# Cross attention: a step's second rounding of queries and keys ahead of the second exponentials, and both remainders in a row

## The chip, the cores and the metric

The kernel runs on one core of one Trainium2 chip. The metric is the time of one execution on the device, in microseconds (us).

## The reference

One transformer block on x (32 batches of 256 tokens, width 256) with a context of 32 x 256 tokens of width 192, all in float32:

```python
h = _layernorm(x, ln1_g, ln1_b)
x = _attention(h, h, sa_wq, sa_wk, sa_wv, sa_wo, sa_bo) + x
h = _layernorm(x, ln2_g, ln2_b)
x = _attention(h, cond_emb, ca_wq, ca_wk, ca_wv, ca_wo, ca_bo) + x
h = _layernorm(x, ln3_g, ln3_b)
p = h @ ff_w1 + ff_b1
a, gate = (p[..., :D_FF], p[..., D_FF:])
h = a * jax.nn.gelu(gate, approximate=False) @ ff_w2 + ff_b2
return h + x
```

`_attention` has 16 heads of 64: q, k and v are projections, the softmax of q k / 8 over the 256 keys weighs v, and the result goes through wo.

## The kernel before

**Rounds and steps.** Each engine has its program written out by hand, and semaphores tie them together. The kernel runs 32 rounds of self attention (`sa`), one for each batch, then 32 of cross attention (`ca`), then the feed-forward part. A round t has four steps, n = 0 to 3, and a step attends to two pairs of heads, pairs 2n and 2n+1. Rounds overlap: while round t ("cur") computes its scores, the output projection of batch t-1 ("prv") and the first projections of batch t+1 ("nxt") are done too. `STEP_UNITS` says which projections (units) stand in which step:

```python
    ((("v", 0, 0), "cur"), (("qk", 2), "cur"), (("qk", 3), "cur"), (("v", 0, 1), "cur")),
    ((("qk", 4), "cur"), (("qk", 5), "cur"), (("wo", 0), "prv")),
    ((("v", 1, 0), "cur"), (("x",), "nxt"), (("qk", 6), "cur"), (("qk", 7), "cur"), (("v", 1, 1), "cur")),
    ((("qk", 0), "nxt"), (("qk", 1), "nxt"), (("wo", 1), "prv")),
```

So every step projects two pairs of queries and keys, and the scores of the next step need both.

**Precision.** A float32 product is made of three products of rounded parts. Each operand is split into its rounding (`_hi`, taken by ScalarE's copy into fp32r) and the remainder (`_lo`, a subtraction on VectorE or GpSimd). For queries and keys: TensorE leaves them in a PSUM bank of `unit_ps`, ScalarE writes `qk_hi` (L887), VectorE `qk_lo` (L1054).

**A step, engine by engine.**

- TensorE: scores of both pairs (`scores`, L605; it waits for the remainders of both pairs), the step's units (`run_unit`, L592), then the weighted sum of an earlier step's values (`attend`, L617).
- VectorE (`attention_iteration` from L1130 on): maximum of the first pair (L1029), transpose of the previous step's second pair (L1043), maximum of the second pair, inverse of the first pair's sums (L1034), remainder of an earlier attended result (L1049), remainder of the first projected pair (L1054), in some steps norm statistics or the transpose of rows (L1020), inverse of the second pair's sums, remainder of the second projected pair (L1054), transpose of this step's first pair. At the end of step 2 come the remainders of the next batch's normed input hT (`x_remainder`, L1067) and of the context's first half (`context_remainder`, L1071, cross attention only). Both subtract one SBUF tensor from another.
- ScalarE: rounding of an earlier attended result (L858), exponentials of the first pair (L849, four rows each with its sum), the units "evacuated early" (`evacuated_early`: the first two of the qk and v units in an even step, the first in an odd one), exponentials of the second pair, the other units. Step 1 ends with the scaling of rows_in to hT (L840) and the norm (L827), step 2 with the copies of context and hT (L874, L876). In each step it issues four of the 16 moves of blocks (L865).
- GpSimd: normalises each pair's probabilities when its sums are inverted (L1259), once in a round the second half of the context's remainder (L1268), behind the normalisation of pair 5, and small work.
- SyncE issues the DMAs: for each step 12 moves of `blocks` to `pT` (L522), behind both transposes of that step (its wait is at L519; the second pair's transpose stands in the next step of VectorE), and once in a round the loads of ctx_in, rows_in and x_res and the stores of x_out and of the rows. rows_in (L507) is the normed input of the next batch, transposed through DRAM. In cross attention's rounds 34 to 36 four loads of feed-forward weights are added.

Of the kernel before, what the change touches and what calls it, by code (L numbers as in the profile page):

```python
# [46 lines left out]
STEP_UNITS = (  # L47
# [5 lines that stand above are left out]
# [44 lines left out]
def attended_before(t, n, parts):  # L97

    if n:
        return attended(t, n - 1, parts)  # L100
    return (t - 1, 1) if "prv" in parts else None
# [58 lines left out]
def block_kernel(nc, x, ctx, ln1_g, ln1_b, ln2_g, ln2_b, ln3_g, ln3_b, sa_wq, sa_wk, sa_wv, sa_wo, sa_bo,  # L160
# [4 lines left out]
    with stack:  # L165
# [170 lines left out]
        ca = Pass("ca", 1, x_sa, x_ca, True, (ca_wq, ca_wk, ca_wv, ca_wo), B, 4)  # L336
# [4 lines left out]
        def pass_of(b, home):  # L341

            return home if not isinstance(b, int) else sa if b < B else ca
# [62 lines left out]
        def norms(t, parts, home):  # L406

            if parts == FILL:
                return [(at, sa, 0, 0)]
            if parts == START:  # L410
                return [(at, sa, 1, 0), (at, sa, 2, 2)]
            if parts == LAST:
                return [(ff, ff, 0, 0)]
            return [] if isinstance(t, int) and t + 2 >= TOTAL else [(at, pass_of(t + 2, home), t + 2, 0)]
# [368 lines left out]
        def _(act):  # L783
# [70 lines left out]
            def attended_hi(b, n):  # L854
                act.wait_ge(at.o_full, b * STEPS + n + 1)
                if n % 2 == 0:
                    at_least(act, at.wo_full, 2 * b - 2 + n // 2 + 1)
                nc.scalar.copy(a_hi[:, 2 * n:2 * n + 2, :], o_ps[:]).then_inc(at.a_hi_done, 1)  # L858
# [16 lines left out]
                act.wait_ge(at.h_done, b + 1)  # L875
                nc.scalar.copy(hT_hi[:, 0, :, :], hT[:]).then_inc(at.x_hi, 1)  # L876

            def evacuated_early(n):

                return [unit for unit in STEP_UNITS[n] if unit[0][0] in ("qk", "v")][:2 if n % 2 == 0 else 1]  # L880

            def split_unit(t, unit, part):
                b = batch_of(t, part)
# [27 lines left out]
            def end_attention():  # L911
                last = TOTAL - 1
                attended_hi(last, 1)
                act.wait_ge(at.qk_full, TOTAL * PAIRS)
                split_ff_weight(0)
                move_blocks(last, 3, ca)
                split_ff_weight(1)
                act.wait_ge(at.v_full, 4 * TOTAL)
                rows_hi(0, 0)
                split_ff_weight(2)  # L920
                attended_hi(last, 2)
                act.wait_ge(param_ld, PARAMS)
                gelu(0, 0)
                gelu(0, 1)
                hidden_hi(0, 0)
                attended_hi(last, 3)

            def attention_iteration(t, parts, home):
                if parts == DRAIN:
                    end_attention()  # L930
                    return
                for sems, ph, b, s in norms(t, parts, home):
                    if s == 0 and parts != FILL:
                        load_rows(sems, ph, b)
                for n in range(STEPS):
                    units = [unit for unit in STEP_UNITS[n] if unit[1] in parts]
                    if behind := attended_before(t, n, parts):
                        attended_hi(*behind)
                    if n == 3 and parts == FILL:
                        split_inputs(t + 1, home)  # L940
                    for p in hi_first(t, n):
                        split_piece(p)
                    if "cur" in parts:
                        exponentials(t, 2 * n)
                    for unit in units:
                        if unit in evacuated_early(n):
                            split_unit(t, *unit)
                    if "cur" in parts:
                        exponentials(t, 2 * n + 1)
                    for unit in units:  # L950
                        if unit not in evacuated_early(n):
                            split_unit(t, *unit)
                    if n == 1 and blocks_next(t, parts):
                        scale_rows(t + 1, home)
                    for sems, ph, b, s in norms(t, parts, home):
                        if n == (2 if isinstance(t, int) and t == 1 else s + 1):
                            if sems is ff:

                                act.wait_ge(at.row_blocks, TOTAL - WHOLE)
                            normalise(sems, b)  # L960
                        if n == 1 and s == 2:
                            load_rows(sems, ph, b)
                    if n == 2 and "nxt" in parts and parts != FILL:
                        split_inputs(t + 1, home)
                    if ready := moved(t, n, parts):
                        move_blocks(*ready, home)
                    for p in hi_last(t, n):
                        split_piece(p)
# [17 lines left out]
        def _(dve):  # L986
# [145 lines left out]
            def attention_iteration(t, parts, home):  # L1132
                if parts == DRAIN:
                    end_attention()
                    return
                if isinstance(t, int) and t == 1:
                    dve.wait_ge(param_ld, PARAMS)

                    for a in (ln_gain, ln_bias):
                        nc.vector.tensor_scalar(a[:, ca.norm, :], a[:, ca.norm, :], SCALE, None, ALU.mult).then_inc(rows_scaled, 1)  # L1140
                for n in range(STEPS):
                    pairs = [(batch_of(t, part), unit[1]) for unit, part in STEP_UNITS[n] if unit[0] == "qk" and part in parts]
                    for sems, ph, b, s in norms(t, parts, home):
                        if n == s + 1:
                            dve.wait_ge(sems.bn_done, b + 1)
                    if "cur" in parts:
                        maxima(t, 2 * n)
                    if behind := moved(t, n, parts):
                        transpose_blocks(behind[0], 2 * behind[1] + 1, home)
                    if "cur" in parts:  # L1150
                        maxima(t, 2 * n + 1)
                    for sems, ph, b, s in norms(t, parts, home):
                        if n == s + 1:
                            norm_moments(sems)
                    if n == 3 and parts == FILL:
                        x_remainder(t + 1)
                    if parts != FILL:
                        for p in lo_vector(t, n):
                            split_queries(p)
                    if "cur" in parts:  # L1160
                        invert_sums(t, 2 * n)
                    if n == 2 and "nxt" in parts and by_tensor(t + 1):
                        if parts == FILL:
                            dve.wait_ge(norm_ld, 16 * 2)
                        scale_inputs(t + 1, home)
                    if behind := attended_before(t, n, parts):
                        attended_lo(*behind)
                    for pair in pairs[:1]:
                        qk_remainders(*pair)
                    for sems, ph, b, s in norms(t, parts, home):  # L1170
                        if n == s:
                            norm_statistics(sems, b)
                    if n == 3 and blocks_ahead(t, parts):
                        transpose_rows(at, t + 2)
                    if "cur" in parts:
                        invert_sums(t, 2 * n + 1)
                    for pair in pairs[1:]:
                        qk_remainders(*pair)
                    if "cur" in parts:
                        transpose_blocks(t, 2 * n, home)  # L1180
                    if n == 2 and "nxt" in parts and parts != FILL:
                        x_remainder(t + 1)
                        if pass_of(t + 1, home).has_ctx:
                            context_remainder(t + 1)
                    if n % 2 and "prv" in parts:
                        project_out(t - 1, n // 2)
                    if parts == FILL:
                        for p in lo_vector(t, n):
                            split_queries(p)
# [160 lines left out]
```

## Time and profile before

| | |
|---|---|
| median of 3 runs | 2939.59 us (2935.07 to 2942.47) |
| profiled execution, own time | 2934.73 us |
| its span | 2932.9 us |
| TensorE busy | 2880.7 us, 98% |
| VectorE busy | 2278.4 us, 78% |
| ScalarE busy | 1911.4 us, 65% |
| GpSimd busy | 1472.5 us, 50% |
| mean granted TensorE clock | 0.996 |

The profile is one execution. Its page gives each engine's busy share, the queues, the chain of work that ended last and the costliest groups of instructions. The views of the trace used below are the timeline (each row: start and duration in us, engine, line, operation, output<-inputs, how many; in brackets the idle time ahead of it and what ended it), and the waits (who waited for whom, us in total, how often, the longest). "PE" is TensorE, "DVE" VectorE, "ACT" ScalarE, "POOL" GpSimd; "SPq" and "ACTq" are DMA issues of SyncE and ScalarE. The duration of an issue is the time in which it holds its sequencer, not that of the transfer. Ends of matmuls are modelled, so TensorE is read by starts.

### The profile page before, as it was taken

To read this page: it belongs to the slowest core of one execution; us is meant where nothing else is said; L and a number is where in the kernel's file an instruction comes from. 1 tells how busy PE (TensorE), PEld (TensorE's weight loads), DVE (VectorE), ACT (ScalarE), POOL (GpSimd) and SP (SyncE) were. 2 spreads that over 40 slices of the span, in tenths; PEclk is the share of its full clock that TensorE was granted. 3 is DMA by queue.
4 is the path that set the end of the run, shared out by engine and by line. 5 is a ranking of instruction groups with operands and counts; after the bars stand their busy time and mean duration, and the time that the engine had idled before them with its cause. 6 is when DMAs were issued, how large, how long until landed. Compare 5 with 4: busy or idle time off the path is not lost.

```text
span 2932.9 us, 76346 instructions
## 1 busy us (share of the span) xinstructions
PE 2880.7 (98%) x25278; PEld 2510.3 (86%) x25278; DVE 2278.4 (78%) x3495; ACT 1911.4 (65%) x6041; POOL 1472.5 (50%) x1310
## 2 busy tenths in 40 slices
PE   8999999999999999999999999999999999999999
PEld 7878888888888888887888888888888889999999
DVE  6878888888888888887888888888888865555554
ACT  6667766666666677876777777777777754444443
POOL 5444444444444444754555555555555545455454
PEclk9999999999999999999999999999999999999999
DMA  5665555555555555566656656666665532222222
GB/s 145 168 170 155 149 149 149 149 149 150 147 147 149 149 149 149 152 164 175 166 159 159 161 159 161 161 161 162 161 162 160 152 109 72 86 75 73 88 72 62
DMA packets 535575, 413.37 MB, mean 141 GB/s; under 512 B 171201, under 2 KB 520769, under 8 KB 535489
## 3 DMA queue, kind: packets, MB, share of 16 engines
q1 hardware_dynamic: 443424, 328.31, 41.1%
q10 hardware_dynamic: 92064, 83.96, 11.2%
q8 instruction: 48, 0.79, 0.1%
q14 instruction: 39, 0.31, 0.0%
HBM read 94.52 MB, written 49.02 MB: 49 GB/s over the span
## 4 chain that ended last, share of the span: by engine, by line
PE 58%; SPq 14%; ACT 12%; DVE 8%; issue 5%; ACTq 3%; DMA 1%; DVEq 0%; POOL 0%; POOLq 0%
PE unit_ps L592 31%; SPq L522 12%; PE s_ps L592 12%; PE o_ps L617 8%; ACT probs L849 8%; PE s_ps L605 7%; ACTq L865 3%; DVE blocks L1043 3%; DVE neg_max L1029 3%; ACT qk_hi L887 3%; DVE hT_lo L1071 1%; DVE hT_lo L1067 1%; DVE qk_lo L1054 1%; ACT x_n L827 1%; DMA rows_in<-rows_t_dram 1%
## 5 line engine op out<-in xcount | busy, mean ns | idle before, releaser
L1259 POOL TENSOR_TENSOR probs<-probs,row_inv 128x1024 f32<-128x1024 f32 x512 | 967.7, 1895 | 956.8 <-DVE row_inv L1034 956.7
L849 ACT ACTIVATE probs<-s_ps,neg_max 128x256 f32<-128x256 f32 x2048 | 952.8, 491 | 266.2 <-DVE neg_max L1029 265.9
L1029 DVE TENSOR_REDUCE neg_max<-s_ps 128x4 f32<-128x1024 f32 x512 | 615.7, 1203 | 72.0 <-PE s_ps L605 71.4
L1043 DVE STREAM_TRANSPOSE blocks<-probs 128x1024 f32<-128x1024 f32 x512 | 632.4, 1235 | 21.3 <-POOL probs L1259 20.9
L592 PE MATMUL unit_ps<-hT_hi,w_hi 128*128 128x256 f32 x2048 | 572.6, 283 | 2.1 <-DVE hT L1024 1.6
L592 PE MATMUL unit_ps<-hT_hi,w_lo 128*128 128x256 f32 x2048 | 555.4, 277 | 0.0
L617 PE MATMUL o_ps<-pT,v_f 128*64 128x256 f32 x4096 | 501.8, 387 | 5.8 <-DMA pT<-blocks 4.6
L592 PE MATMUL unit_ps<-hT_lo,w_hi 128*128 128x256 f32 x1792 | 497.0, 277 | 0.0
L849 ACT ACTIVATION_READ_ACCUMULATOR probs<-s_ps,neg_max 128x1 f32 x2048 | 450.9, 220 | 0.0
L592 PE MATMUL unit_ps<-w_hi,a_hi 128*128 128x256 f32 x1536 | 438.3, 285 | 1.4 <-POOL a_lo L1274 1.0
L592 PE MATMUL unit_ps<-w_hi,a_lo 128*128 128x256 f32 x1536 | 435.0, 283 | 0.0
L592 PE MATMUL unit_ps<-w_lo,a_hi 128*128 128x256 f32 x1536 | 429.9, 280 | 0.0
L1054 DVE TENSOR_TENSOR qk_lo<-unit_ps,qk_hi 128x512 fp32r<-128x512 f32 x512 | 352.6, 689 | 99.4 <-ACT qk_hi L887 95.3
L617 PEld LDWEIGHTS o_ps<-pT,v_f 128*64 128x64 f32 x4096 | 272.8, 137 | 182.2 <-issue 49.4
L592 PEld LDWEIGHTS unit_ps<-hT_hi,w_hi 128*128 128x128 f32 x2048 | 385.1, 188 | 20.7 <-DVE hT L1024 2.0
L592 PEld LDWEIGHTS unit_ps<-hT_hi,w_lo 128*128 128x128 f32 x2048 | 385.0, 188 | 0.0
L858 ACT CAST a_hi<-o_ps 128x512 fp32r<-128x512 f32 x256 | 150.4, 588 | 339.9 <-issue 138.7
L592 PEld LDWEIGHTS unit_ps<-hT_lo,w_hi 128*128 128x128 f32 x1792 | 336.9, 188 | 5.7
L605 PE MATMUL s_ps<-qk_hi 64*128 64x256 f32 x2048 | 316.7, 305 | 20.7 <-DVE qk_lo L1054 18.2
L1274 POOL TENSOR_TENSOR a_lo<-probs,a_hi 128x256 fp32r<-128x256 f32 x256 | 190.0, 747 | 266.7 <-ACT a_hi L905 265.0
L900 ACT ACTIVATE probs<-s_ps,b_col 128x256 f32<-128x256 f32 x256 | 121.8, 476 | 303.4 <-PE s_ps L592 303.4
L887 ACT CAST qk_hi<-unit_ps 128x512 fp32r<-128x512 f32 x512 | 315.0, 615 | 3.7 <-PE unit_ps L592 3.6
(73 smaller groups left out, 6009.7 us busy)
## 6 DMA issues: line engine op xcount, KB each, us to landing
pT<-blocks SPq DMA_DIRECT2D x3072, 64.0 KB, 2.0
pT<-blocks ACTq DMA_DIRECT2D x1024, 64.0 KB, 2.1
rows_t_dram<-row_blocks SPq DMA_DIRECT2D x91, 256.0 KB, 2.4
rows_in<-rows_t_dram SPq DMA_DIRECT2D x91, 256.0 KB, 2.9
x_res<-in_x_dram SPq DMA_DIRECT2D x32, 256.0 KB, 2.7
x_sa_dram<-x_out SPq DMA_DIRECT2D x32, 256.0 KB, 2.2
x_ln<-x_sa_dram ACTq DMA_DIRECT2D x32, 256.0 KB, 3.2
ctx_in<-in_ctx_dram SPq DMA_DIRECT2D x32, 256.0 KB, 2.8
```

The source lines that it names most:

```text
L522: sp.dma_start(pT[j * BLK:(j + 1) * BLK, n % 2, :, i, :], blocks[i * BLK:(i + 1) * BLK, n % 2, :, j, :]).then_inc(landed(b, n, home)[0], 16)
L592: last = nc.tensor.matmul(dst, a, b, start=start and n == 0, stop=stop and n == len(terms) - 1)
L605: last = nc.tensor.matmul(s_ps[:, m % 2, hd, it * S:(it + 1) * S], q[part, r, 0, rows], k[part, r, 1, :], start=n == 0, stop=n == 2)
L617: last = nc.tensor.matmul(o_ps[part, i, :], v_f[:, jt, 2 * (2 * n + i) + hd, :], p[:, jt, hd], start=jt == 0, stop=jt == IT - 1)
L849: op = nc.scalar.activation(probs[:, m % 2, r, :], s_ps[:, m % 2, r // IT, r % IT * S:(r % IT + 1) * S], ACT.Exp, bias=neg_max[:, m % RING ...
L858: nc.scalar.copy(a_hi[:, 2 * n:2 * n + 2, :], o_ps[:]).then_inc(at.a_hi_done, 1)
L887: nc.scalar.copy(qk_hi[:, unit[1] % RING, :, :], bank.rearrange("p (a s) -> p a s", a=2)).then_inc(at.qk_hi, 1)
L1029: nc.vector.tensor_reduce(neg_max[:, m % RING, :], s_ps[:, m % 2, :, :].rearrange("p h (i j) -> p (h i) j", j=S), AX_X, ALU.max, negate=Tr ...
L1043: nc.vector.transpose(blocks[:, n % 2, m % 2, :, :].rearrange("p b (j r c) -> p r j b c", j=IT, c=BLK), probs[:, m % 2, :, :].rearrange("p ...
L1054: nc.vector.tensor_tensor(qk_lo[:, m % RING, :, :], unit_ps[:, bank_of(("qk", m)), :].rearrange("p (a s) -> p a s", a=2), f32(qk_hi[:, m % ...
L1259: nc.gpsimd.tensor_tensor(probs[:, m % 2, :, :], probs[:, m % 2, :, :], row_inv[:, m % RING, :].unsqueeze(2).broadcast_to([P, ROWS, S]), A ...
L1274: nc.gpsimd.tensor_tensor(a_lo[:, m, :], hid[:, m % 2, :], f32(a_hi[:, m, :]), ALU.subtract).then_inc(ff.u_lo, 1)
```

## The change

In rounds of cross attention, one more qk unit counts as early. ScalarE rounds the second projected pair of a step behind the first and ahead of the second exponentials; VectorE takes the remainder of the second pair right behind that of the first, ahead of norm statistics, the transpose of rows and the inverse of the second pair's sums. Self attention is left as it is, and so are TensorE, GpSimd and SyncE. Behind L878 line numbers grow by two, and by three in what follows the second edit.

```diff
@@ -875,9 +875,11 @@
-            def evacuated_early(n):
-
-                return [unit for unit in STEP_UNITS[n] if unit[0][0] in ("qk", "v")][:2 if n % 2 == 0 else 1]
+            def evacuated_early(t, n, home):
+
+
+                units = [unit for unit in STEP_UNITS[n] if unit[0][0] in ("qk", "v")]
+                return units[:(2 if n % 2 == 0 else 1) + (1 if pass_of(t, home) is ca else 0)]
@@ -1165,7 +1167,8 @@
-                    for pair in pairs[:1]:
+                    early = 2 if "cur" in parts and pass_of(t, home) is ca else 1
+                    for pair in pairs[:early]:
                         qk_remainders(*pair)
@@ -1174,7 +1177,7 @@
-                    for pair in pairs[1:]:
+                    for pair in pairs[early:]:
                         qk_remainders(*pair)
```

ScalarE in step 2 of a cross attention round, behind the exponentials of pair 4, before (the register instructions hold a value to wait for):

```order
L893 COPY v_f<-unit_ps 128x512
L886 REGISTER_ALU
L887 CAST qk_hi<-unit_ps 128x512
L849 ACTIVATE probs,row_sum<-s_ps,neg_max 128x256 x4
L886 REGISTER_ALU
L887 CAST qk_hi<-unit_ps 128x512
L891 REGISTER_ALU
L893 COPY v_f<-unit_ps 128x512
```

and now:

```order
L895 COPY v_f<-unit_ps 128x512
L888 REGISTER_ALU
L889 CAST qk_hi<-unit_ps 128x512
L888 REGISTER_ALU
L889 CAST qk_hi<-unit_ps 128x512
L849 ACTIVATE probs,row_sum<-s_ps,neg_max 128x256 x4
L893 REGISTER_ALU
L895 COPY v_f<-unit_ps 128x512
```

The second rounding (pair 7) has moved ahead of the four exponentials of pair 5; v stays behind them.

VectorE in the same step, from the remainder of an attended result (`a_lo`) to the remainder of the next input (`hT_lo`), before:

```order
L1049 TENSOR_TENSOR a_lo<-o_ps,a_hi 128x512
L1053 REGISTER_ALU
L1054 TENSOR_TENSOR qk_lo<-unit_ps,qk_hi 128x512
L1034 RECIPROCAL row_inv<-row_sum 128x4
L1053 REGISTER_ALU
L1054 TENSOR_TENSOR qk_lo<-unit_ps,qk_hi 128x512
L1042 ISA
L1043 STREAM_TRANSPOSE blocks<-probs 128x4x2x4x32
L1066 REGISTER_ALU
L1067 TENSOR_TENSOR hT_lo<-hT,hT_hi 128x512
```

and now:

```order
L1051 TENSOR_TENSOR a_lo<-o_ps,a_hi 128x512
L1055 REGISTER_ALU
L1056 TENSOR_TENSOR qk_lo<-unit_ps,qk_hi 128x512
L1055 REGISTER_ALU
L1056 TENSOR_TENSOR qk_lo<-unit_ps,qk_hi 128x512
L1036 RECIPROCAL row_inv<-row_sum 128x4
L1044 ISA
L1045 STREAM_TRANSPOSE blocks<-probs 128x4x2x4x32
L1068 REGISTER_ALU
L1069 TENSOR_TENSOR hT_lo<-hT,hT_hi 128x512
```

The remainder of the second pair has moved ahead of the inverse of the second sums, which now stands right in front of the transpose of the first pair (`blocks`).

## Rows read from the trace of the kernel before

**Rows 1.** TensorE timeline, cross attention, step ends: start us, us, engine, line, op.
```profile
1705.56 1.95 PE L617 MATMUL o_ps<-pT,v_f 128*64 128x256 f32 x16
1707.44 0.39 PE L605 MATMUL s_ps<-qk_hi 64*128 64x256 f32 x2
...
1714.10 1.95 PE L617 MATMUL o_ps<-pT,v_f 128*64 128x256 f32 x16
1716.27 0.39 PE L605 MATMUL s_ps<-qk_hi 64*128 64x256 f32 x2 [0.23 <-DVE qk_lo L1054]
...
1732.24 1.95 PE L617 MATMUL o_ps<-pT,v_f 128*64 128x256 f32 x16
1734.41 0.38 PE L605 MATMUL s_ps<-qk_hi 64*128 64x256 f32 x2 [0.22 <-DVE qk_lo L1054]
```

**Rows 2.** SyncE's queue, one round of cross attention, timeline.
```profile
1702.87 0.39 SPq L512 DMA_DIRECT2D ctx_in<-in_ctx_dram  x1
1703.46 0.37 SPq L507 DMA_DIRECT2D rows_in<-rows_t_dram  x1
1704.03 15.94 SPq L522 DMA_DIRECT2D pT<-blocks  x24
1720.18 0.42 SPq L543 DMA_DIRECT2D x_res<-x_sa_dram  x1
1721.17 7.97 SPq L522 DMA_DIRECT2D pT<-blocks  x12
...
1738.91 0.39 SPq L512 DMA_DIRECT2D ctx_in<-in_ctx_dram  x1
```

**Rows 3.** Waits of SyncE, 1200 to 2365 us: total, times, longest us.
```profile
SPq L519 <- DVE blocks L1043: 13.9, 28, 1.7
```

**Rows 4.** SyncE's queue, timeline of a round that also loads feed-forward weights.
```profile
1334.81 0.46 SPq L512 DMA_DIRECT2D ctx_in<-in_ctx_dram  x1
...
1373.86 0.46 SPq L512 DMA_DIRECT2D ctx_in<-in_ctx_dram  x1
```

**Rows 5.** ScalarE timeline, step 1's end and step 2 of cross attention.
```profile
1706.75 0.64 ACT L840 ACTIVATE hT<-rows_in,ln_bias,ln_gain 128x256 f32<-128x256 f32 x1 [1.27 <-DMA rows_in<-rows_t_dram]
...
1710.27 0.48 ACT L849 ACTIVATE probs<-s_ps,neg_max 128x256 f32<-128x256 f32 x1
...
1713.02 0.53 ACT L849 ACTIVATE probs<-s_ps,neg_max 128x256 f32<-128x256 f32 x1
...
1714.84 0.65 ACT L887 CAST qk_hi<-unit_ps 128x512 fp32r<-128x512 f32 x1
...
1715.30 0.67 ACT L893 COPY v_f<-unit_ps 128x512 f32<-128x512 f32 x1
...
1716.30 0.71 ACT L876 CAST hT_hi<-hT 128x512 fp32r<-128x512 f32 x1
```

**Rows 6.** VectorE timeline, end of step 2 and start of step 3.
```profile
1716.13 1.24 DVE L1043 STREAM_TRANSPOSE blocks<-probs 128x1024 f32<-128x1024 f32 x1
1717.29 0.65 DVE L1067 TENSOR_TENSOR hT_lo<-hT,hT_hi 128x512 fp32r<-128x512 f32 x1
1717.86 0.96 DVE L1071 TENSOR_TENSOR hT_lo<-ctx_in,hT_hi 128x256 fp32r<-128x256 f32 x1
1718.73 1.21 DVE L1029 TENSOR_REDUCE neg_max<-s_ps 128x4 f32<-128x1024 f32 x1
1719.87 1.23 DVE L1043 STREAM_TRANSPOSE blocks<-probs 128x1024 f32<-128x1024 f32 x1
```

**Rows 7.** GpSimd timeline, same stretch.
```profile
1715.30 1.90 POOL L1259 TENSOR_TENSOR probs<-probs,row_inv 128x1024 f32<-128x1024 f32 x1 [0.91 <-DVE row_inv L1034]
1717.36 1.18 POOL L1268 TENSOR_TENSOR hT_hi<-ctx_in,hT_hi 64x256 fp32r<-64x256 f32 x1 [0.16 <-POOL probs L1259]
```

**Rows 8.** Timeline of VectorE and GpSimd near the start of self attention.
```profile
45.47 2.37 POOL L1254 TENSOR_TENSOR w_lo<-w_stage,w_hi 128x1024 fp32r<-128x1024 f32 x1
...
45.89 2.50 DVE L1067 TENSOR_TENSOR hT_lo<-hT,hT_hi 128x512 fp32r<-128x512 f32 x1
```

More of the change, by code:

```diff
@@ L945, in attention_iteration @@
                     for unit in units:
-                        if unit in evacuated_early(n):
+                        if unit in evacuated_early(t, n, home):
                             split_unit(t, *unit)
@@ L950, in attention_iteration @@
                     for unit in units:
-                        if unit not in evacuated_early(n):
+                        if unit not in evacuated_early(t, n, home):
                             split_unit(t, *unit)
```

## The prediction

> **What bounds the kernel now.** The change touches only the 32 rounds of cross attention (one per batch, some 36 us each, four steps a round, n = 0 to 3), so I read that stretch engine by engine and asked which engine is never idle there.
>
> First TensorE, because the page shows it as the busiest. A step ends with the attend product (L617) and the next begins with the scores (L605). Where nothing is waited for, the scores start 1.88 us behind the attend (1707.44 less 1705.56). At two other step ends they start 2.17 us behind it, and the wait printed there is for qk_lo, the remainder that VectorE takes last in a step [rows 1]. That is 0.29 us twice a round. The fourth step end shows no wait as long as these, so I count it between 0 and 0.29 and take the middle. TensorE loses some 0.58 + 0.15 = 0.73 us a round for remainders that come late. This is what the change goes after, and 32 x 0.73 = 23.4 us is what it could give if TensorE set the pace.
>
> Second SyncE's queue, because each step moves its transposed blocks by 12 DMAs from there. One round lies between two ctx_in loads: 1738.91 - 1702.87 = 36.04 us. In it the issues stand one behind the other, with gaps of 0.20 us (1703.83 to 1704.03), except one: from the end of the x_res issue, 1720.60, to 1721.17 there are 0.57 us, so SyncE waits 0.37 [rows 2]. The wait view names what for: VectorE's blocks (L1043), 28 times in cross attention, 13.9 us in all, and nothing else [rows 3]. SyncE thus has 36.04 - 0.37 = 35.67 us of its own work a round, and TensorE without its waits would need 36.04 - 0.73 = 35.31. **SyncE, not TensorE, is the longer.** A second sign: a round that has four more loads on SyncE lasts 1373.86 - 1334.81 = 39.05 us [rows 4], though no engine computes anything more in it.
>
> Third, what the one wait of SyncE hangs on. It is a ring. SyncE issues rows_in at 1703.46 [rows 2]; ScalarE has been idle for it and scales it at 1706.75, issues its own four moves and starts the exponentials of pair 4 at 1710.27 [rows 5]. Then follow, without idle time, two roundings, the exponentials of pair 5 (1713.02), the rounding of pair 7 (1714.84), v (1715.30), and the copies of context and hT (the last from 1716.30) [rows 5]. VectorE subtracts hT's rounding at 1717.29, then the context's, takes the maximum of pair 6 at 1718.73 and transposes pair 5 at 1719.87, to 1721.10 [rows 6]. SyncE goes on at 1721.17 [rows 2], and after fixed work comes to the next rows_in. Nothing of TensorE's sets a time in this ring. So a round is SyncE's work plus how late that transpose of pair 5 comes, counted from rows_in.
>
> **The change, part by part.**
>
> (1) ScalarE in step 2: the rounding of pair 7 goes ahead of the exponentials of pair 5. It occupied the slot 1714.84 to 1715.30, 0.46 us [rows 5]. The exponentials start 0.46 later, and v and everything behind it stay where they are, since the same work stands ahead of them. Steps 3, 0 and 1 get the same swap, but it only moves work inside stretches where ScalarE waits for VectorE or rows_in at the next step's start; I cost it at nothing, the cover being ScalarE's idle time (1.27 us ahead of rows_in) [rows 5]. If the cover goes, each step costs up to 0.46.
>
> (2) VectorE takes both remainders in a row, in time in which it waited for the exponentials. In step 2 the transpose of pair 4 then no longer stands behind the remainder of pair 7. It starts as soon as the later sums are inverted, some 0.5 us sooner than at 1716.13. TensorE's waits of [rows 1] go.
>
> (3) What this does for the ring. hT's remainder was held by that transpose, not by its input: ScalarE's copy ended at 1716.30 + 0.71 = 1717.01 [rows 5], VectorE began at 1717.29 [rows 6]. Read this far, the remainder could start at about 1717.06, 0.23 sooner, and every round would be 0.23 shorter.
>
> (4) What stands against it. GpSimd normalises pair 5 when its sums are inverted, from 1715.30 to 1717.20, and the remainder began 0.09 us behind its end [rows 6, 7]. With the exponentials 0.46 later, GpSimd works from 1715.76 to 1717.66, across 1717.06. Do the two work at the same time? The trace has such a case: at 45.89 the same instruction at L1067 meets a GpSimd subtraction that runs from 45.47 to 47.84. It lasts 2.50 us in place of 0.65, and ends at 48.39, 0.55 behind GpSimd [rows 6, 8]. The context's remainder shows the same in every round: 256 columns take 0.96 us where 512 take 0.65, and they end at 1718.82, 0.28 behind GpSimd's own context instruction (1717.36 + 1.18 = 1718.54) [rows 6, 7]. So the two take turns. The Trainium skill, "SBUF — State Buffer", section "Who interferes with whom", says that a VectorE instruction with two SBUF inputs contends with a GpSimd instruction that reads SBUF, and that the one that comes second blocks for the whole instruction. The trace agrees with it (2.50 us in place of 0.65). By that rule the ring gets longer; without it, it would get 0.23 us shorter.
>
> The sum for a round: hT's remainder is held to 1717.66, ends at 1717.66 + 0.55 = 1718.21 instead of 1717.94, which is **0.27 us later**. GpSimd's context instruction waits for it, VectorE's context remainder waits for that, as now, so the maximum of pair 6, the transpose of pair 5 and SyncE's next move are all 0.27 later. SyncE's wait grows from 0.37 to 0.64.
>
> For the kernel: the 28 rounds with a wait of SyncE for that transpose [rows 3] give 28 x 0.27 = 7.6 us. In the others SyncE is late anyway and covers it. TensorE's 23.4 us are not paid out: it comes to its next product earlier and waits there, since SyncE's pace holds rows_in and with it v. Only behind the last round can it keep a little of its lead, about one step end's wait or two; I take 0.6. Sum: +7.0 us on the profiled execution's own 2934.73, so 2941.7, a quarter of a per cent. The median of the runs shown, 2939.59, lies 4.9 us above that execution; the same +7.0 there gives **2946.6 us**. What a measurement of this kernel can tell from no change is about 0.3%, 8.8 us: my forecast is no change that can be told, on the slow side.
>
> Bounds of the unknown. The price of the turn-taking lies between -0.23 (none) and +0.43 a round (below), the nearest row being the 2.50 us of [rows 8], which is the same instruction, so I take its 0.55.
>
> **Rivals.**
>
> *The remainder runs beside the normalisation.* Then part (3) holds: 28 x 0.23 = 6.4 us less, 2933.2. It can't give more than SyncE's whole wait, 13.9 us [rows 3]. For it: the GpSimd instruction of [rows 8] is another than the normalisation. Against it: both read two tensors. Chance 0.15.
>
> *TensorE sets the pace after all.* Then all waits of [rows 1] are gained: 2939.6 - 23.4 = 2916.2. For it: 98% busy on the page, the waits are real, and SyncE's issues could shrink. Against it: [rows 2 to 4]. Chance 0.06.
>
> *Slower beyond doubt.* GpSimd's context instruction follows its normalisation by 0.16 us [rows 7]. If it gets its turn ahead of the waiting remainder, it runs from 1717.82 for the 0.60 that it takes alone (1718.54 less 1717.94), to 1718.42; then hT's remainder to 1718.97, the context's to 1719.25 instead of 1718.82, 0.43 later. 28 x 0.43 = 12.0 us: 2951.6. What decides is who gets in within those 0.16 us; the waiting one should. Chance 0.12.
>
> *The halves cancel and nothing moves*: 2939.6, chance 0.07. The diff moves exactly what it names, so I give nothing to its not doing so.
>
> **How the numbers follow.** The forecast has 0.60. The range takes in the first rival, the forecast and the third with the spread of the runs shown (some 3.7 us to either side): 2929 to 2955; the TensorE case stays outside. Faster by over 0.3%: 0.06, and a third of the first rival, together 0.11. Slower by over 0.3%: nearly all of the third rival and a fifth of the forecast, 0.24. The rest, 0.65, is within.
>
> **What would show it.** In the profile after: no wait of the scores for qk_lo in cross attention; TensorE idle instead ahead of the v product, for ScalarE's v_f. The remainder of hT recorded at some 1.2 us instead of 0.65, ending 0.55 behind GpSimd's normalisation. Rounds of 36.3 us. SyncE's waits for blocks some 0.64 each. If hT's remainder stays at 0.65 and rounds are 35.8, step (4) is wrong; if rounds are 35.3, the reading of SyncE is wrong; if SyncE has no wait and rounds are longer, its issues got slower, which I did not foresee.

## The result and the profile after

| | before | after |
|---|---|---|
| median of 17 runs each | 2939.55 us (2935.07 to 2945.67) | 2947.96 us (2942.78 to 2951.2) |
| ratio after/before, 95% interval | | 1.0027 (1.002 to 1.0033) |
| span of the profiled execution | 2932.9 us | 2943.5 us |
| granted TensorE clock | 0.996 | 0.997 |
| mean round, rows_in to rows_in, 1450 to 2250 us (22 rounds before, 21 after) | 36.01 us | 36.29 us |

The kernel got slower, by a little less than the 0.3% that I took as what can be told; with 17 runs on each side the interval excludes 1. The forecast was 2946.6.

SyncE's queue in one round after, the answer to [rows 2] (columns: start, duration, engine and line, operation, number of issues):

```profile
1709.63 0.39 SPq L512 DMA_DIRECT2D ctx_in<-in_ctx_dram  x1
1710.22 0.37 SPq L507 DMA_DIRECT2D rows_in<-rows_t_dram  x1
1710.79 15.90 SPq L522 DMA_DIRECT2D pT<-blocks  x24
1726.90 0.42 SPq L543 DMA_DIRECT2D x_res<-x_sa_dram  x1
1728.18 7.88 SPq L522 DMA_DIRECT2D pT<-blocks  x12
...
1745.84 0.39 SPq L512 DMA_DIRECT2D ctx_in<-in_ctx_dram  x1
```

The only hole is again behind x_res: 1728.18 - (1726.90 + 0.42) = 0.86 us, of which 0.20 is the usual gap. SyncE waits 0.66 us where it waited 0.37. The round is 1745.84 - 1709.63 = 36.21 us.

VectorE in that step, the answer to [rows 6] (in brackets the idle time ahead and what ended it):

```profile
1722.23 0.18 DVE L1036 RECIPROCAL row_inv<-row_sum 128x4 f32<-128x4 f32 x1 [1.04 <-ACT probs L849]
1722.38 1.25 DVE L1045 STREAM_TRANSPOSE blocks<-probs 128x1024 f32<-128x1024 f32 x1
1723.75 1.18 DVE L1069 TENSOR_TENSOR hT_lo<-hT,hT_hi 128x512 fp32r<-128x512 f32 x1
1724.86 0.96 DVE L1073 TENSOR_TENSOR hT_lo<-ctx_in,hT_hi 128x256 fp32r<-128x256 f32 x1
1725.74 1.21 DVE L1031 TENSOR_REDUCE neg_max<-s_ps 128x4 f32<-128x1024 f32 x1
1726.87 1.23 DVE L1045 STREAM_TRANSPOSE blocks<-probs 128x1024 f32<-128x1024 f32 x1
```

and GpSimd, the answer to [rows 7]:

```profile
1722.49 1.89 POOL L1262 TENSOR_TENSOR probs<-probs,row_inv 128x1024 f32<-128x1024 f32 x1 [1.39 <-DVE row_inv L1036]
1724.54 0.99 POOL L1271 TENSOR_TENSOR hT_hi<-ctx_in,hT_hi 64x256 fp32r<-64x256 f32 x1 [0.16 <-POOL probs L1262]
```

hT's remainder now begins at 1723.75, inside the normalisation (1722.49 to 1724.38). It lasts 1.18 us instead of 0.65 and ends at 1724.93, 0.55 us behind the normalisation's end, as the case in [rows 8] did. GpSimd's context instruction, VectorE's context remainder, the maximum and the transpose of pair 5 follow. Counted from the start of the exponentials of pair 4, the steady rounds show GpSimd's normalisation of pair 5 starting 0.48 us later (5.52 instead of 5.04), hT's remainder starting 0.24 sooner (6.78 instead of 7.02) and the maximum of pair 6 starting 0.29 later (8.76 instead of 8.47). The end of the remainder goes with the end of the normalisation: it lies 0.55 us behind it now and lay 0.74 behind it before, so of the 0.48 us there remain 0.29.

TensorE at a step's end and ahead of v, the answer to [rows 1]:

```profile
1711.57 1.95 PE L617 MATMUL o_ps<-pT,v_f 128*64 128x256 f32 x16
1713.45 0.38 PE L605 MATMUL s_ps<-qk_hi 64*128 64x256 f32 x2
...
1719.44 0.50 PE L592 MATMUL unit_ps<-w_hi,hT_hi 128*128 128x512 f32 x1 [0.43 <-ACT v_f L895]
```

The scores now start 1.88 us behind the attend product, the undisturbed distance of [rows 1], at every step end of cross attention but two. Summed over all step ends, what the distance exceeds its least fell from some 21 us to under 0.1. That leaves out one step end before (0.93 us) and two after (1.18 us each), all in rounds that also load feed-forward weights: there the attend product itself takes 2.88 and 3.13 us instead of 1.95. None of this reached the time: TensorE waits ahead of v instead. The waits of TensorE and of SyncE's queue from 1450 to 2250 us, 22 rounds (columns: total, times, longest), after:

```profile
PE unit_ps L592 <- ACT v_f L895: 11.8, 22, 0.9
...
SPq L519 <- DVE blocks L1045: 16.1, 22, 1.3
```

and the same rows before:

```profile
PE s_ps L605 <- DVE qk_lo L1054: 8.9, 42, 0.2
...
PE unit_ps L592 <- ACT v_f L893: 0.2, 1, 0.2
...
SPq L519 <- DVE blocks L1043: 9.7, 22, 1.0
```

SyncE's total wait grew by 6.4 us in 22 rounds, 0.29 a round.

Where the 10.6 us between the two profiled spans lie follows from SyncE's ctx_in loads (starts of the first round's, the seventh's and a late one's; before, then after):

```profile
1184.85 0.59 SPq L512 DMA_DIRECT2D ctx_in<-in_ctx_dram  x1
...
1412.76 0.39 SPq L512 DMA_DIRECT2D ctx_in<-in_ctx_dram  x1
...
2278.68 0.39 SPq L512 DMA_DIRECT2D ctx_in<-in_ctx_dram  x1
```

```profile
1186.35 0.59 SPq L512 DMA_DIRECT2D ctx_in<-in_ctx_dram  x1
...
1418.00 0.39 SPq L512 DMA_DIRECT2D ctx_in<-in_ctx_dram  x1
...
2290.09 0.39 SPq L512 DMA_DIRECT2D ctx_in<-in_ctx_dram  x1
```

Ahead of cross attention +1.5 us (nothing is changed there; in the seven other profiled kernels that leave ctx_in's load on SyncE this stretch ends between 1182.4 and 1186.8 us, so I take it for the spread between executions); six early rounds 231.65 instead of 227.91, +3.7; 24 steady rounds 872.09 instead of 865.92, +6.2, or 0.26 each; behind them -0.8.

### The profile page after: what moved, and what is told of

The parts are those of the page before. It is cut to its first block, busy times and chain, and to the rows that moved or that the text cites. A ratio compares the mean times of both kernels' runs of the same rounds, so it can differ in the third digit from the quotient of the medians.

```text
span 2943.5 us, 76346 instructions
## 1 busy us (share of the span) xinstructions
PE 2884.1 (98%) x25278; PEld 2510.7 (85%) x25278; DVE 2290.2 (78%) x3495; ACT 1909.9 (65%) x6041; POOL 1465.2 (50%) x1310
## 4 chain that ended last, share of the span: by engine, by line
PE 50%; SPq 23%; ACT 8%; issue 7%; DVE 4%; DMA 3%; ACTq 3%; POOL 2%; POOLq 0%; DVEq 0%
PE unit_ps L592 26%; SPq L522 20%; PE s_ps L592 12%; PE o_ps L617 7%; PE s_ps L605 6%; ACT probs L849 4%; DMA rows_in<-rows_t_dram 2%; ACTq L865 2%; DVE blocks L1045 2%; DVE neg_max L1031 1%; ACT qk_hi L889 1%; POOL probs L1262 1%; DVE hT_lo L1073 1%; ACT x_n L827 1%; ACT v_f L895 1%
## 5 line engine op out<-in xcount | busy, mean ns | idle before, releaser
L1056 DVE TENSOR_TENSOR qk_lo<-unit_ps,qk_hi 128x512 fp32r<-128x512 f32 x512 | 341.0, 685 | 62.8 <-ACT qk_hi L889 58.8
L1090 DVE SCALAR_TENSOR_TENSOR probs<-s_ps,b_col,probs 128x256 f32<-128x256 f32 x256 | 123.3, 482 | 244.7 <-ACT probs L902 242.5
```

Source lines behind the costliest of these rows:

```text
L1056: nc.vector.tensor_tensor(qk_lo[:, m % RING, :, :], unit_ps[:, bank_of(("qk", m)), :].rearrange("p (a s) -> p a s", a=2), f32(qk_hi[:, m % ...
L1090: nc.vector.scalar_tensor_tensor(hid[:, m % 2, :], s_ps[:, m % 4 // 2, m % 2, 0:S], b1_col[:, m:m + 1], gate[:, m % 2, :], ALU.add, ALU.mu ...
```

## The experiments

The theory was the ring of the prediction, lengthened by the turn-taking of hT's remainder with GpSimd's normalisation. The rivals: the longer rounds come from another of the four steps, or SyncE is not what sets the pace. The times of before in the four groups of runs were 2936.98 (first three kernels), 2939.33 (next four), 2940.17 (next four) and 2940.76 us (last). All ratios are to before.

**Is step 2 the place? The change in steps 3, 0 and 1 alone, and in step 2 alone.** In the functions of the edit, for the first (`n == 2` for the second):

```diff
-                return units[:(2 if n % 2 == 0 else 1) + (1 if pass_of(t, home) is ca else 0)]
+                return units[:(2 if n % 2 == 0 else 1) + (1 if pass_of(t, home) is ca and n != 2 else 0)]
...
-                    early = 2 if "cur" in parts and pass_of(t, home) is ca else 1
+                    early = 2 if "cur" in parts and pass_of(t, home) is ca and n != 2 else 1
```

> The change in steps 0, 1 and 3 of cross attention alone; step 2 as before. Theory (the price comes from step 2, where GpSimd's normalisation of pair 5 slides across VectorE's remainder of hT): nothing in the ring moves, rounds of 36.0 us, SyncE's wait 0.37, hT's remainder 0.65 long; time as the kernel before, ratio 0.999 to 1.001. Rival (each step that swaps its second rounding pays for the later exponentials): three quarters of the loss of 8 us, ratio about 1.002.

Measured: 2929.6 us, ratio 0.9975 (0.9964 to 0.9986), mean round 35.74 us. No lengthening, as expected, but a gain of 7.4 us where I expected none.

> The change in step 2 alone. Theory: the whole loss, rounds of 36.3 us, hT's remainder recorded at some 1.2 us, ratio 1.002 to 1.004. Rival (every step pays its part): a quarter of the loss, ratio about 1.0007.

Measured: 2945.98 us, ratio 1.0032 (1.002 to 1.0043), mean round 36.37, SyncE's wait 16.7 us in 22 rounds. The whole loss is in step 2. The two halves don't add up: -7.4 + 9.0 = +1.6 us, and the full change costs 8.4. The mean rounds say the same: -0.27 and +0.36 us alone, +0.28 together.

**Is it the turn-taking?** In cross attention the remainder of hT reads, in place of the SBUF tensor hT, the PSUM bank of pair 7. In this kernel hT_lo is therefore not hT's remainder; engine, shape, place in the order and the waits of the other engines are the same.

```diff
+                if home is not None and pass_of(b, home).has_ctx:
+                    nc.vector.tensor_tensor(hT_lo[:, 0, :, :],
+                                            unit_ps[:, bank_of(("qk", 7)), :].rearrange("p (a s) -> p a s", a=2),
+                                            f32(hT_hi[:, 0, :, :]), ALU.subtract).then_inc(at.x_lo, 1)
+                    return
                 nc.vector.tensor_tensor(hT_lo[:, 0, :, :], hT[:], f32(hT_hi[:, 0, :, :]), ALU.subtract).then_inc(at.x_lo, 1)
```

> The change whole, but in cross attention VectorE's remainder of hT takes its first input from a PSUM bank (what the projection of pair 7 left there) instead of from hT, so that it has one SBUF input; its size is the same. The remainder it writes is therefore not that of hT. Theory (two SBUF inputs and GpSimd take turns): it starts at 6.78 us behind the exponentials of pair 4 as in the changed kernel and now lasts 0.65 us beside the normalisation; the context's remainder gets in right behind the normalisation; the maximum of pair 6 comes some 0.8 us sooner than in the kernel before (7.6 to 7.7 instead of 8.47), SyncE's wait goes, rounds fall to SyncE's own 35.7 us: ratio 0.996 to 0.998. Rival (the later normalisation or the later exponentials delay the ring in another way): it stays at 1.002 to 1.003.

Measured: 2920.79 us, ratio 0.9946 (0.9932 to 0.9959), mean round 35.38: a larger gain than expected. VectorE:

```profile
1712.93 1.25 DVE L1045 STREAM_TRANSPOSE blocks<-probs 128x1024 f32<-128x1024 f32 x1
1714.30 0.69 DVE L1070 TENSOR_TENSOR hT_lo<-unit_ps,hT_hi 128x512 fp32r<-128x512 f32 x1
1714.91 0.42 DVE L1078 TENSOR_TENSOR hT_lo<-ctx_in,hT_hi 128x256 fp32r<-128x256 f32 x1
1715.24 1.22 DVE L1031 TENSOR_REDUCE neg_max<-s_ps 128x4 f32<-128x1024 f32 x1
```

and GpSimd:

```profile
1713.05 1.90 POOL L1267 TENSOR_TENSOR probs<-probs,row_inv 128x1024 f32<-128x1024 f32 x1 [1.39 <-DVE row_inv L1036]
1715.10 0.82 POOL L1276 TENSOR_TENSOR hT_hi<-ctx_in,hT_hi 64x256 fp32r<-64x256 f32 x1 [0.16 <-POOL probs L1267]
```

The same subtraction over the same normalisation (1713.05 to 1714.95) lasts 0.69 us and ends at 1714.99, when only one of its inputs is in SBUF. That is the rule of the Trainium skill named in the prediction ("SBUF — State Buffer", "Who interferes with whom"), which limits it to two SBUF inputs; 0.69 against 1.18 us agrees with it. The context's remainder, which reads ctx_in and hT_hi from SBUF, also falls from 0.96 to 0.42: it now begins at 1714.91, ahead of GpSimd's context instruction (1715.10), and now it is that one that waits: it ends 0.59 us behind the end of VectorE's (1715.92 less 1715.33), its 0.60 alone, and is recorded at 0.82 us. SyncE's queue:

```profile
1700.15 0.39 SPq L512 DMA_DIRECT2D ctx_in<-in_ctx_dram  x1
...
1717.46 0.42 SPq L543 DMA_DIRECT2D x_res<-x_sa_dram  x1
1718.07 7.67 SPq L522 DMA_DIRECT2D pT<-blocks  x12
...
1735.52 0.39 SPq L512 DMA_DIRECT2D ctx_in<-in_ctx_dram  x1
```

From x_res (ends 1717.88) to the moves there is the usual 0.19, no wait, and the round is 35.37 us. The gain is larger than the two waits of the ring allowed, since SyncE's own work came out at 35.3 to 35.4 and not at the 35.67 of the prediction. Its 12 moves take 7.67 us where they took 7.97 [rows 2] and 7.88.

**Where does the gain of steps 3, 0 and 1 come from? Step 3 alone** (`n == 3` in both conditions):

> The change in step 3 alone. The run of steps 0, 1 and 3 gained 0.28 us a round though SyncE's wait stayed at 0.36: SyncE's issue some 19.5 us behind rows_in took 0.84 there before and 0.60 in that run, and ScalarE's issue beside it began 0.04 us ahead of it before and 0.09 behind it in that run. Theory (who issues second pays, and step 3 sets who is second): the whole gain is in step 3, rounds of 35.7 us, ratio 0.997 to 0.998. Rival (TensorE's shorter waits for remainders in steps 0 and 1 give it): ratio 1.000.

Measured: 2931.99 us, ratio 0.9976 (0.9966 to 0.9985), mean round 35.81. The whole gain is there. In the kernel with steps 3, 0 and 1, SyncE's queue shows where:

```profile
1702.29 0.39 SPq L512 DMA_DIRECT2D ctx_in<-in_ctx_dram  x1
...
1703.45 15.83 SPq L522 DMA_DIRECT2D pT<-blocks  x24
1719.49 0.42 SPq L543 DMA_DIRECT2D x_res<-x_sa_dram  x1
1720.46 7.65 SPq L522 DMA_DIRECT2D pT<-blocks  x12
...
1737.89 0.39 SPq L512 DMA_DIRECT2D ctx_in<-in_ctx_dram  x1
```

SyncE's wait is as before (0.97 - 0.42 - 0.20 = 0.35 us), but the moves behind it take 7.65 us instead of 7.97. In that stretch ScalarE issues its own moves of the same form. Before, one issue of SyncE and one of ScalarE's beside it:

```profile
1723.10 0.84 SPq L522 DMA_DIRECT2D pT<-blocks  x1
...
1723.05 0.62 ACTq L865 DMA_DIRECT2D pT<-blocks  x1
```

With steps 3, 0 and 1 changed:

```profile
1722.38 0.60 SPq L522 DMA_DIRECT2D pT<-blocks  x1
...
1722.46 0.80 ACTq L865 DMA_DIRECT2D pT<-blocks  x1
```

An issue of these moves takes 0.60 us on SyncE and 0.62 on ScalarE undisturbed. Where two meet, one of them may pay some 0.2 us. In this meeting it is SyncE before, which has no time to spare; with ScalarE's exponentials and issues later in step 3 it is ScalarE, which has.

One pair of issues is an example only, so I counted all of these moves between 1450 and 2250 us. Before, two begin within 0.2 us of each other 151 times. In 78 of these meetings neither lasts over 0.70 us; in 71 the one that began second does, and in the other two ScalarE's does, which began 0.01 us ahead. After, there are 126 meetings, and in 59 the second pays, in none the first. The 12 moves behind x_res take 7.95 us in the mean of the rounds before and 7.66 with steps 3, 0 and 1 changed, 0.30 less; the rounds are 0.27 us shorter.

**A wait added and nothing else.** If that reading holds, the kernel before must get faster by a wait alone. Ahead of ScalarE's moves in step 3 stands one more wait, for the exponentials of pairs 0 to 5 of the round. Those are long done in step 3, so the wait holds nothing back; its own instruction can only make the issues a little later:

```diff
+                    if n == 3 and "cur" in parts and pass_of(t, home) is ca:
+                        act.wait_ge(at.exp_done, t * PAIRS + 6)
```

> The kernel before with one more wait ahead of ScalarE's four moves in step 3 of cross attention, on a semaphore that is long fulfilled; it can only delay these issues by some 0.05 to 0.15 us. Theory (who issues second pays): ScalarE's second move begins behind SyncE's issue, so ScalarE's takes 0.8 and SyncE's 0.64 instead of 0.84, rounds of 35.7 to 35.8 us, ratio 0.997 to 0.999, from a wait added and nothing taken out. Rival (the order of ScalarE's and VectorE's work gave the gain): ratio 1.000.

Measured: 2934.79 us, ratio 0.9982 (0.9973 to 0.999), mean round 35.84; the 12 moves take 7.65 us in the mean and the pair of issues reads:

```profile
1724.69 0.60 SPq L522 DMA_DIRECT2D pT<-blocks  x1
...
1724.67 0.80 ACTq L865 DMA_DIRECT2D pT<-blocks  x1
```

ScalarE's issue begins 0.02 us ahead of SyncE's instead of 0.05, and it is the one that pays. A wait added to one engine shortens the kernel by 5.4 us, as predicted from the issues. Not all of the 0.30 us that the moves gain reaches the round (0.17): SyncE's wait grew from 9.7 to 14.4 us in 22 rounds. In the full change the two meet again the bad way round. Step 2's longer wait makes SyncE's issues later as well:

```profile
1730.10 0.76 SPq L522 DMA_DIRECT2D pT<-blocks  x1
...
1729.95 0.62 ACTq L865 DMA_DIRECT2D pT<-blocks  x1
```

so SyncE pays 0.16 us here again, and its 12 moves take 7.87 us in the mean (7.96 with step 2 alone). Of the 0.30 us that they gained in step 3's kernels 0.22 are given back. The halves miss the whole by 0.2 us a round, so this is the reading I have for why they don't add up; no run holds step 2's shift and the good order of issues at once to prove it.

**Cutting the ring at other places.** ScalarE's four moves in step 1, which stand between rows_in and the exponentials of pair 4, go ahead of its scaling of the rows, in which it otherwise waits for rows_in:

```diff
+                    ahead = n == 1 and "cur" in parts and pass_of(t, home) is ca
+                    if ahead:
+                        move_blocks(t, 0, home)
...
-                    if ready := moved(t, n, parts):
+                    if not ahead and (ready := moved(t, n, parts)):
```

In the kernel before:

> The kernel before; in cross attention ScalarE issues its four moves of step 0's blocks ahead of the scaling of rows_in, in its idle time, instead of behind it. Theory (ring through rows_in, with SyncE's own 35.67 us as the floor): the exponentials of pair 4 start up to 0.54 us sooner behind rows_in (then the maximum of pair 4 holds them), which is more than SyncE's wait of 0.37, so that wait goes and rounds are 35.7 us: some 10 us less, ratio 0.996 to 0.998. Rival (TensorE's waits for remainders set the pace): rounds stay at 36.0, ratio 1.000.

Measured: 2932.81 us, ratio 0.9978 (0.9969 to 0.9987), mean round 35.82. In the changed kernel:

> The changed kernel with the same edit. Theory: the 0.29 us of the remainder's turn and more is taken off the ring, SyncE never waits, rounds of 35.7 us as in the run beside it: ratio 0.996 to 0.998 to the kernel before, although TensorE has no wait for remainders and that other kernel has. Rival (SyncE is no floor): rounds of 35.3 us, ratio about 0.992.

Measured: 2932.31 us, ratio 0.9971 (0.996 to 0.9982), mean round 35.69. The changed kernel gains more (its ratio falls from 1.0027 to 0.9971) than the one before does (to 0.9978), as a longer ring should. But the rounds were expected at 35.7 in both with no wait of SyncE left, and in 22 rounds it still waits 4.9 us (before) and 9.0 (changed). Part is given back: rows_in now lands some 3.6 us (changed) and 4.0 us (before) behind its issue instead of 3.2 and 3.1.

Then SyncE is relieved as well: ctx_in's load, one of its issues a round, is given to ScalarE at the round's start.

```diff
-                if "nxt" in parts and (ph := pass_of(t + 1, home)).has_ctx:     # in SyncE's program
-                    load_context(ph, t + 1)
...
+                if "nxt" in parts and (ph := pass_of(t + 1, home)).has_ctx:     # in ScalarE's
+                    load_context(ph, t + 1)
```

Both edits in the kernel before, and in the changed one:

> The kernel before, with ScalarE's moves ahead of rows_in and the load of ctx_in issued by ScalarE at the round's start instead of by SyncE (0.6 us off SyncE: 35.1 us of own work a round). Theory: SyncE is no longer the longest; now TensorE's waits for remainders count. Rounds between 35.3 and 35.9 us, most likely 35.6: ratio 0.994 to 0.997.

Measured: 2920.07 us, ratio 0.9933 (0.9919 to 0.9947), mean round 35.40, a little better than expected.

> The changed kernel with both edits. Theory: TensorE sets the pace with 35.3 us a round and no wait for remainders, some 22 us less than the kernel before, ratio 0.991 to 0.994, and faster than the run beside it by what the change is worth once SyncE is out of the way (0.3 us a round, some 8 us). Rival (the change costs by itself, whatever the ring): slower than the run beside it.

Measured: 2921.15 us, ratio 0.9939 (0.9926 to 0.9953), mean round 35.42. The ratio came as expected, the lead over the kernel before it did not: with SyncE relieved the two are equal. In this one pair 7's rounding waits for TensorE (the first exponentials of pair 4, that rounding, and the meeting on GpSimd and VectorE):

```profile
1739.10 0.47 ACT L847 ACTIVATE probs<-s_ps,neg_max 128x256 f32<-128x256 f32 x1 [0.19 <-DVE neg_max L1034]
...
1742.41 0.59 ACT L887 CAST qk_hi<-unit_ps 128x512 fp32r<-128x512 f32 x1 [0.42 <-PE unit_ps L586]
...
1745.12 1.89 POOL L1265 TENSOR_TENSOR probs<-probs,row_inv 128x1024 f32<-128x1024 f32 x1 [1.74 <-DVE row_inv L1039]
...
1746.38 1.18 DVE L1072 TENSOR_TENSOR hT_lo<-hT,hT_hi 128x512 fp32r<-128x512 f32 x1
```

The exponentials of pair 5 come about 0.5 us later, and GpSimd's normalisation with them (6.02 to 7.91 behind the exponentials of pair 4, instead of 5.52 to 7.41), so hT's remainder, at 7.28, still meets it. That this is all that holds the kernel back is not shown.

**The better version.** The change in steps 3, 0 and 1, which gained, with both edits:

> The change in steps 0, 1 and 3 with both other edits (ScalarE's moves ahead of rows_in, ctx_in loaded by ScalarE). TensorE's floor is 35.3 us a round; the kernel before with both edits has 35.4 and the whole change with both 35.43. Expected 35.3, ratio 0.992 to 0.993, that is at most 3 us below the kernel before with both edits. A ratio under 0.991 would mean that 35.3 is no floor.

Measured: 2913.45 us, ratio 0.9911 (0.9898 to 0.9923), more than expected. From one rows_in to the next:

```profile
1730.13 0.38 SPq L507 DMA_DIRECT2D rows_in<-rows_t_dram  x1
...
1765.32 0.39 SPq L507 DMA_DIRECT2D rows_in<-rows_t_dram  x1
```

35.19 us a round, with TensorE busy 799.85 of 800 us between 1450 and 2250 (before 788.69). That share alone does not say that TensorE sets the pace, since the ends of its matmuls are modelled: in the changed kernel with the moves ahead it is busy 799.69 us, at 35.69 us a round. The starts say more. Counted from start to start, the projections and the scores take the same here as in the kernel before with both edits, to 0.01 us a round, and the attend product with what follows it 7.51 us instead of 7.73. That is 0.22 of the 0.23 us by which the rounds differ (35.17 and 35.40 in the mean), so once SyncE is relieved the waits for late remainders are paid.

Which of the two edits does it? The kernel before with ctx_in's load on ScalarE alone, and steps 3, 0 and 1 with it alone:

> The kernel before with ctx_in loaded by ScalarE alone. It takes 0.6 us off SyncE's work between the wait for pair 5's transpose and the next rows_in, which is in the ring, and nothing off ScalarE's way from rows_in. Theory: rounds of 35.4 to 35.5 us, ratio 0.993 to 0.995. If ScalarE's moves ahead of rows_in were what gained most in the run with both edits, the ratio stays near 0.998.

Measured: 2919.45 us, ratio 0.9932 (0.9919 to 0.9945), mean round 35.44: the same as with both edits.

> The change in steps 0, 1 and 3, and ctx_in loaded by ScalarE; ScalarE's moves stay behind rows_in. The run with the moves ahead too came to 35.2 us a round and ratio 0.9911; the load alone to 35.4 and 0.9932. If the moves ahead of rows_in matter once SyncE is relieved, this lies at 0.993; if they don't, at 0.991.

Measured: 2913.86 us, ratio 0.9907 (0.989 to 0.9923). So the load does it, and the moves ahead add nothing once SyncE has time. This last kernel, the change without step 2 and one load on another queue, is the simpler of the two that beat both kernels: 26.9 us under the 2940.76 of before in its group.

## Why the prediction was right, and where it was off

**The bound.** Right. TensorE's 23.4 us (measured some 21) went and were not paid out, and [rows 2 to 4] showed why: moving one 0.4 us issue off SyncE, with nothing done about TensorE's waits, gained 20.7 us.

**Part (1), the roundings.** In step 2 as said. The cost "at nothing" for steps 3, 0 and 1 is the term that failed. As compute it was right, the cover was there. But ScalarE also issues DMAs in those steps, and I did not ask what its issues meet when they come later. Alone that is worth -7.4 us (-8.2 in the kernel with step 3 alone), all in step 3. In the full change most of it is gone again, by the phase that step 2 gives SyncE's issues, as I read it. So the result agreed with the zero by an interplay that I had not seen: that part of the agreement is luck.

**Parts (2) and (3).** Right: hT's remainder starts 0.24 us sooner; forecast 0.23.

**Part (4), the turn-taking.** Right in mechanism and size: 1.18 us, ending 0.55 behind the normalisation, 0.29 us a round where 0.27 was forecast, SyncE's wait 0.66 where it was 0.64. What made the round longer is not the sooner start of the remainder but the later end of the normalisation that it has to let pass. The experiment with one SBUF input turned the loss into a gain at the same place in the order. What was not tried is to avoid the meeting without altering what is computed.

**The sum.** +7.0 forecast, +8.4 measured between the medians. The steady rounds gave 6.2 for 24. The six early rounds, where SyncE was to cover it "anyway", gave 3.7 in the two profiled executions and not 0. Nearly all of it, 3.5, lies in the three rounds that also load feed-forward weights. No run looks into these. The kernel before with nothing but the added wait also has 229.67 us in these six rounds, 1.8 more than 227.91, so a part can be spread between executions. The lead kept at the end was put at 0.6, and the profiles show 0.8.

**Constants that weren't.** SyncE's 35.67 us of own work is not fixed: as long as it issues ctx_in's load it was 35.2 to 35.7 across these kernels (mean round less mean wait), and the moves behind x_res, which meet ScalarE's, make 0.3 of that. And the 35.31 us of TensorE was too much: the round of 35.19 lies below it. Neither decided this forecast, but both would have decided one about a change that relieves SyncE.

**The rivals.** The remainder does not run beside the normalisation at its full speed. TensorE does not set the pace until SyncE is relieved. GpSimd's context instruction did not get in first: recorded from 1724.54, it ended at 1725.53, 0.60 us behind the remainder's end at 1724.93, which is what the prediction gave it alone.

## What to carry to other kernels

An engine that computes nothing can be the one that sets the pace: add up the issues of a DMA queue over one round and look for the one hole in it, before believing the busiest engine. When an instruction with two SBUF inputs on VectorE is freed to start sooner, look at what GpSimd does at that moment, and at whether the same change makes GpSimd later: here the instruction ended 0.55 us behind GpSimd's, whenever that was. And when work is shifted on an engine that also issues DMAs, lay its issues beside those of the other queues, since a shift of 0.03 to 0.13 us there was worth 5 to 8 us, about as much as the whole change.

## What the runs showed of the hardware that I had not expected

- Issues of SyncE and ScalarE delay each other. Alone they take 0.60 and 0.62 us; where two meet, SyncE's took 0.76 or 0.84, or ScalarE's 0.80. About half of the meetings within 0.2 us cost nothing (78 of 151 before); where one pays, it is the one that begins second (SyncE's by 0.05 and 0.15 us, ScalarE's by 0.08). In the kernel with the added wait both are recorded within 0.02 us of each other and ScalarE paid. What inside the issue path does this, the traces don't show.
- With ScalarE's four issues moved to where SyncE issues ctx_in and rows_in, rows_in landed 4.0 us behind its issue instead of 3.1 (3.6 instead of 3.2 in the changed kernel). This is no rule about issues side by side: in the kernel before with both edits the four begin 0.54 to 2.47 us behind rows_in, ctx_in's load is no longer ahead of it, and it lands in 2.8. Which of these makes the difference no run separates.
- The waiting VectorE instruction gets its turn in the 0.16 us between two GpSimd instructions: GpSimd's context instruction ended 0.60 us behind the end of hT's remainder, and not ahead of it.
